# An attention-and-feed-forward chain on one core: another written-out order of all engines in the third stage

## The reference

```
hq, hk, hv = q @ Wq, k @ Wk, v @ Wv            # 16 heads of 64
attn = hq.hk + shift(hq.head_r) + hk.ub + shift(head_r.vb)   # content + relative part
attn = softmax(where(mask, -INF, attn / sqrt(128)))
out = (attn @ hv) * sigmoid(q @ head_w)
out = out @ Wo + q ;  out = layernorm(out) * ln_g + ln_b
```

## The kernel before, in words

| block | what | tile | line |
|---|---|---|---|
| hq0, hq1 | queries of heads 0-7, 8-15 | 128x128 | L1189, L1221 |
| hk0, hk1 | keys of heads 0-7, 8-15 | 128x128 | L1177, L1321 |
| hv0, hv1 | values | 128x120 | L1232, L1181 |
| z, xnT | head gate; transpose of the normed x | 128x128 | L1280, L1329 |
| rel 0..3 | relative scores of head pairs 0-1, 2-3, 4-5, 6-7 | 64x32 | L1244, L1274, L1304, L1347 |
| content 0, 1 | queries times keys, heads 0-7, 8-15 | 64x128 | L1258, L1213 |
| T0, T1 | transposes of the probabilities, half the heads each | 64x120 | L1205, L1315 |
| av | probabilities times values, four groups | 120x64 | L1169, L1287, L1292, L1355 |
| y | output product, in two halves | 128x128 | L1195, L1227 |
| qT, acc | transpose and product of part 4, 16-bit | 128x128 | L1251, L1334 |

## Time and profile before

### The profile page before, as it was taken

The page is one execution under the profiler, slowest core; times in us unless marked ns, Lnnn a source line. Parts: engine busy times, 40 slices in busy tenths (PEclk is TensorE's granted clock), DMA queues, the critical chain, the costliest instruction groups (busy, mean ns, idle before and its releaser), DMA issues.

```text
span 460.4 us, 16745 instructions
## 1 busy us (share of the span) xinstructions
PE 428.4 (93%) x6147; PEld 317.8 (69%) x6147; DVE 384.3 (83%) x1316; ACT 370.7 (81%) x1467; POOL 252.8 (55%) x370
## 2 busy tenths in 40 slices
PE   8999999988779989799999999999999999999781
PEld 7556556555547768577887887888788778787570
DVE  5899999998468985489888989989898998988974
ACT  1999999989724564379899899899889989989961
POOL 4488888878935651023244444553654555355684
PEclk9999999999669999899999999999999999999987
DMA  7150000000000002777566565766746766476100
GB/s 216 51 192 22 14 12 6 10 7 8 1 2 1 0 2 69 190 193 186 127 160 150 126 165 123 161 147 140 180 108 159 155 144 163 120 180 148 29 7 23
DMA packets 54392, 44.88 MB, mean 97 GB/s; under 512 B 43952, under 2 KB 49328, under 8 KB 54320
## 3 DMA queue, kind: packets, MB, share of 16 engines
q1 hardware_dynamic: 53616, 43.59, 38.6%
q10 hardware_dynamic: 704, 0.32, 0.2%
HBM read 22.92 MB, written 20.97 MB: 95 GB/s over the span
## 4 chain that ended last, share of the span: by engine, by line
PE 78%; DVE 11%; ACT 4%; POOL 3%; DMA 1%; issue 1%; SPq 1%; POOLq 0%
PE PS L964 68%; PE PS L1161 4%; PE PS L980 2%; PE PS L1141 2%; POOL prob L307 1%; ACT prob L488 1%; DMA ctx<-in_ctxT 1%; DVE relw L709 1%; DVE nmax L666 1%; DVE nmax L668 1%; DVE relr L714 1%; PE PS L1086 1%; DVE nmax L640 1%; DVE qT L699 1%; DVE probT L647 1%
## 5 line engine op out<-in xcount | busy, mean ns | idle before, releaser
L351 POOL TENSOR_TENSOR prob<-prob,rsum 128x480 f32<-128x480 f32 x64 | 62.6, 989 | 70.7 <-DVE rsum L832 37.4
L488 ACT ACTIVATE prob<-prob,nmax 128x120 f32<-128x120 f32 x256 | 100.3, 414 | 0.0
L417 ACT ACTIVATE prob<-PS,nmax 128x120 f32<-128x120 f32 x256 | 89.4, 394 | 3.3 <-DVE nmax L731 2.9
L307 POOL TENSOR_TENSOR prob<-prob,rsum 128x480 f32<-128x480 f32 x64 | 62.5, 986 | 22.1 <-DVE rsum L704 12.4
L417 ACT ACTIVATION_READ_ACCUMULATOR prob<-PS,nmax 128x1 f32 x256 | 61.7, 241 | 0.0
L488 ACT ACTIVATION_READ_ACCUMULATOR prob<-prob,nmax 128x1 f32 x256 | 56.3, 220 | 0.0
L964 PE MATMUL PS<-rT,qv 64*32 64x152 f32 x2048 | 48.1, 297 | 2.4 <-ACT relw L567 2.4
L964 PE MATMUL PS<-ctx,wk 128*128 128x120 f32 x288 | 43.9, 289 | 2.3 <-DMA ctx<-in_ctxT 2.3
L964 PEld LDWEIGHTS PS<-xnT,wq 128*128 128x128 f32 x288 | 36.8, 191 | 9.3 <-issue 6.8
L964 PEld LDWEIGHTS PS<-rT,qv 64*32 64x32 f32 x2048 | 28.6, 106 | 20.6 <-issue 18.6
L964 PE MATMUL PS<-xnT,wq 128*128 128x128 f32 x288 | 42.5, 285 | 0.0
(11 more groups left out here) (195 smaller groups left out, 1100.6 us busy)
## 6 DMA issues: line engine op xcount, KB each, us to landing
rel_scratch<-relw SPq DMA_DIRECT2D x128, 152.0 KB, 2.7
relr<-rel_scratch SPq DMA_DIRECT2D x64, 240.0 KB, 4.3
ctx<-in_ctxT SPq DMA_DIRECT2D x32, 60.0 KB, 1.9
out_x<-fin SPq DMA_DIRECT2D x16, 64.0 KB, 2.2
x_all<-in_x SPq DMA_DIRECT2D x1, 640.0 KB, 7.1
wr<-in_wr SPq DMA_DIRECT2D x1, 512.0 KB, 5.0
wq<-in_wq SPq DMA_DIRECT2D x1, 512.0 KB, 3.7
wk<-in_wk SPq DMA_DIRECT2D x1, 512.0 KB, 4.5
```

Of the source, the lines that this page charges most:

```text
L307: return pool.tensor_tensor(pr, pr, cols(rsum[p], g, HG).unsqueeze(2).to_broadcast([S, HG, SK]), ALU.mult)
L351: return pool.tensor_tensor(pr, pr, cols(rsum[p], g, HG).unsqueeze(2).to_broadcast([S, HG, SK]), ALU.mult)
L417: last = act.activation(cols(prob[p], n, SK), cols(scores, q, SK), ACT.Exp, bias=nmax[p][:, n:n + 1], accum_out=ssum[p][:, n:n + 1])
L488: last = act.activation(cols(pr, n, SK), cols(pr, n, SK), ACT.Exp, bias=bias[:, n:n + 1], accum_out=total[:, n:n + 1])
```

## The change

Only `layer1` changes, on all five engines, and the number of steps in `run_steps`: the last one is now step 23. Per element PE does the same products with the same tiles. Their order in a step, and with it the number of times that the tile of one block differs from that of the block before, becomes:

| | blocks of one step, in order (element) |
|---|---|
| before | av last quarter (s-4); hk0 (s-1), hv1 (s-2), hq0 (s), y 1st (s-4); T0 (s-3); content 1 (s-2); hq1 (s), y 2nd (s-4), hv0 (s-2); rel 0; qT (s-6); content 0 (s-1); rel 1; z (s-1); av 1st half (s-3); rel 2; T1 (s-3); hk1 (s), xnT (s+1), acc (s-6); rel 3; av third quarter (s-3) |
| after | content 1 (s-2); qT (s-7), hq0 (s), y 1st (s-4); av 2nd half (s-4); hk1 (s-1), z (s-1), hv1 (s-2), hq1 (s), acc (s-7), y 2nd (s-4), xnT (s+1), hk0 (s-1), hv0 (s-2); rel 1, rel 0; T0 (s-3); content 0 (s-1); rel 2, rel 3; av 1st half; T1 (s-3) |

Semicolons stand where the tile changes: round the step that is 15 times before and 10 after with T to content (64x120 to 64x128) counted, 14 and 8 without. Banks are dealt out anew. The copy of keys of heads 8-15 goes from DVE to ACT; ACT's copy of xnT comes one step earlier; DVE norms x one step earlier; part 4 (qT, acc, the copy `fin`) runs on element s-7 instead of s-6 up to the copy, and its result is stored at s-8 instead of s-7. On SP the store of the result moves ahead of the load of the context. Core of the diff:

```diff
-            peeled(layer1, LOOPS[2][1], NB + 7)
+            peeled(layer1, LOOPS[2][1], NB + 8)
...
 # SP: order of the transfers in a step
                     shifted(t, p, 0)
+                t, p = s - 8, par
+                if on(t):
+                    out_at = held(sp, t * S * D)
+                    sp.wait_ge(F1["out"], t + 1)
+                    sp.dma_start(bass.AP(out.tensor, out_at, [[D, S], [1, D]]), fin[p][:, :]).then_inc(F1[f"stored{p}"], 16)
                 t, p = s, par
...
-                    sp.wait_ge(A1["relw1"], t + 1)
+                    sp.wait_ge(A1["relw0"], t + 1)
                     store(t, p, 0)
...
 # ACT
+                    act.wait_ge(A1["hq_ps"], 2 * t + 2)
+                    act.activation(cols(qv[p], 1, 512), PS[:, 2, :], ACT.Identity, bias=vbs_sb[:, :], scale=SCALE1)\
+                        .then_inc(A1["qv1"], 1)
...
+                t, p = s - 1, 1 - par
+                if on(t):
+                    after(act, A1["rsum"], 4 * t - 4)
+                    act.activation(ez[p][:, :], PS[:, 7, 0:H], ACT.Exp, scale=-1.0).then_inc(A1["ez"], 1)
+                    act.activation(cols(kT[p], 1, 4 * SK), PS[:, 5, 0:4 * SK], ACT.Copy).then_inc(A1["kT1"], 1)
...
+                    act.wait_ge(A1["rel_ps"], 4 * t + 1)
+                    act.activation(relw[p][:, 2 * WIN:4 * WIN], PS[:, 3, 0:2 * WIN], ACT.Copy)
+                    act.activation(relw[p][:, 6 * WIN:8 * WIN], PS[:, 4, 0:2 * WIN], ACT.Copy)\
+                        .then_inc(A1["relw1"], 1)
+                    act.wait_ge(A1["rel_ps"], 4 * t + 2)
+                    act.activation(relw[p][:, 0 * WIN:2 * WIN], PS[:, 1, 0:2 * WIN], ACT.Copy)
+                    act.activation(relw[p][:, 4 * WIN:6 * WIN], PS[:, 5, 0:2 * WIN], ACT.Copy)\
+                        .then_inc(A1["relw0"], 1)
...
 # DVE
-                    dve.wait_ge(A1["hk_ps"], 2 * t + 1)
-                    dve.tensor_copy(cols(kT[p], 1, 4 * SK), PS[:, 1, 0:4 * SK]).then_inc(A1["kT1"], 1)
...
 # PE
+                    pe.wait_ge(A1["probT3"], t + 1)
...
+                t, p = s - 1, 1 - par
+                if on(t):
+                    pe.wait_ge(A1[f"ctx_loaded{p}"], loads(t, p))
+                    freed(pe, (A1["probT3"], t - 2, t - 3), (A1["relw2"], t + 1, t))
+                    for m in range(4, 8):
+                        last = mm(PS[:, 5, (m % 4) * SK:(m % 4 + 1) * SK], cols(wk1_sb, m, 2 * DK), ctx_sb[p][:, :])
...
+                    pe.wait_ge(A1["kT0"], t + 1)
+                    freed(pe, (A1["relw1"], t + 2, t + 1), (A1["u"], t - 2, t - 3))
...
+                    pe.wait_ge(A1["relw0"], t + 1)
+                    for m in (4, 5):
...
+                    freed(pe, (A1["probT0"], t - 2, t - 3), (A1["kT0"], t, t - 1))
...
+                    for m in (6, 7):
```

More of the change, by code:

```diff
@@ new lines, in layer1 @@
+                t, p = s + 2, par
+                if on(t):
+                    if isinstance(t, int) and t < 2:
+                        dve.wait_ge(F0["xnT_ps"], NB)
+                    dve.wait_ge(A1["rstd"], t + 1)
+                    after(dve, A1["xn_kept"], t - 1)
+                    dve.tensor_scalar(xn[p][:, :], row(x_all, t), mv[p][:, 0:1], rstd[p][:, 0:1],
+                                      ALU.subtract, ALU.mult).then_inc(A1["xn"], 1)
+                    dve.wait_ge(A1["xn"], t + 1)
+                    dve.tensor_copy(row(xn_all, t), xn[p][:, :]).then_inc(A1["xn_kept"], 1)
@@ new lines, in layer1 @@
+                t, p = s - 1, 1 - par
+                if on(t):
+                    dve.wait_ge(A1["content"], 2 * t + 1)
+                    dve.wait_ge(A1[f"relr0{p}"], 2 * loads(t, p))
+                    dve.tensor_tensor(cols(prob[p], 0, HG * SK), PS[:, 3, 0:HG * SK], cols(relr[p], 0, HG * SK), ALU.add)\
+                       .then_inc(A1["added0"], 1)
+                    dve.tensor_tensor(cols(prob[p], 1, HG * SK), PS[:, 7, 0:HG * SK], cols(relr[p], 1, HG * SK), ALU.add)\
+                       .then_inc(A1["added1"], 1)
@@ L1207, in layer1 @@
-                if on(t):
-                    freed(pe, (A1["kT0"], t + 2, t + 1), (A1["added1"], t + 1, t))
-                    freed(pe, (A1["relw3"], t + 2, t + 1), (A1["added0"], t + 1, t))
-                    for m in range(4, 8):
-                        for e, bank in ((0, 7), (1, 6)):
-                            half_ = slice(e * DK, (e + 1) * DK)
-                            last = mm(PS[:, bank, (m % 4) * SK:(m % 4 + 1) * SK], cols(qu[p], m, S)[half_], cols(kT[p], m, SK)[half_])
-                    last.then_inc(A1["content"], 1)
@@ L1295, in layer1 @@
[L1295 to L1300 removed]
+                    for m in (0, 1):
+                        for e, bank in ((0, 1), (1, 5)):
                             half_ = slice(e * DK, (e + 1) * DK)
@@ new lines, in layer1 @@
+                    pe.wait_ge(A1["scaled0"], ready)
+                    pe.wait_ge(A1["scaled1"], ready)
+                    probs_transpose(p, 0, (6, 0)).then_inc(A1["probT_ps"], 1)
+                t, p = s - 1, 1 - par
+                if on(t):
+                    pe.wait_ge(A1["kT0"], t + 1)
+                    freed(pe, (A1["relw1"], t + 2, t + 1), (A1["u"], t - 2, t - 3))
+                    freed(pe, (A1["hv0"], t, t - 1), (A1["ez"], t + 1, t))
+                    for m in range(0, 4):
+                        for e, bank in ((0, 3), (1, 7)):
+                            half_ = slice(e * DK, (e + 1) * DK)
+                            last = mm(PS[:, bank, (m % 4) * SK:(m % 4 + 1) * SK], cols(qu[p], m, S)[half_], cols(kT[p], m, SK)[half_])
+                    last.then_inc(A1["content"], 1)
@@ L1342, in layer1 @@
                     for m in (6, 7):
-                        for e, bank in ((0, 6), (1, 5)):
+                        for e, bank in ((0, 6), (1, 0)):
                             half_ = slice(e * DK, (e + 1) * DK)
```

570 lines of the change are left out of this document (248 added, 322 removed), and 9 rows, old and new, of the table A1.

## The result

| | before | changed | ratio, 95% interval |
|---|---|---|---|
| first timing, medians of 20 and 20 runs | 464.91 | 459.73 (457.72 to 465.69) | 0.992, 0.989 to 0.995 |
| a later job, 17 and 6 runs | 464.98 | 459.92 (459.53 to 460.75) | 0.989, 0.984 to 0.994 |

The ratio is not the quotient of the two medians, from which it differs by up to 0.6 points (here 0.989 by the medians).

The account below looks back on a forecast made before the run. PE was taken to bound the kernel at 16.31 us a step. Full steps 8.5 plus filling 3.9, emptying 0, made 12.4 off 462.21, so 449.8; with the median 0.4 above, 450 us, range 441 to 458.

Parts of the forecast that it names:

- PE, 15.60 us a step: Steady step: PE's blocks in the new order sum to 15.60 us, 0.71 less, with bounds 15.45 and 15.75.
- The forecast of 8.5 us for the twelve steps: Full steps 4 to 15: twelve times 0.71 us saved, 8.5 us in all.
- ACT, 15.25 and not the bound: Steady step: ACT takes over a 0.50 us copy, 14.75 to 15.25, and fits under 15.60 with 0.35 to spare.
- The two points with 0.1 to 0.2 us in hand: ACT's window copies before content 0 and rel 3: just in time for PE; a miss costs that much a step.
- loses 0.66 ..., keeps some 1.2 us a step free: Steady step: DVE sheds the key copy, 0.66 us (about 0.56 in a packed queue), and has some 1.2 us free.
- POOL is half idle: nothing: Steady step: POOL, busy 8.32 of 16.32 us, was expected to cost nothing.
- SP and `relr1`: SP's queue: the second shifted half waits behind the context load, mostly covered; DVE can be a further 1.5 us late.
- Filling 3.9 and emptying 0: First steps 3.9 us less in sum; last steps 0, from -2 to +2.
- The wait for the second context: Step 1, PE before hk1: 3.05 us for 0.68 of work; hk1 moves to step 2, 5.4 us less, 0.8 back.
- the 1.7 that I allowed for waits that stay: Steps 2 and 3: first scores wait for relr and exponentials whatever PE does, so 1.7 us of saving is given back.
- partly eaten: Rival: the two thin points fail or relr1 costs DVE, 0.3 us a step, filling gives only 1: 456.5 us; chance 0.20.
- ACT becomes the bound: Rival: ACT's work plus remaining waits sets the step, 15.95 to 16.25 us, no gain, 458 to 461.5; 0.11 shared between no-change cases.

Follow-up runs that it names:

- e2: The changed kernel with only DVE's order within a step altered, masks and xf moved away from POOL's scalings: 459.61 us, ratio 0.987.
- e8: The changed kernel with e2's DVE order up to step 15 and its own order from step 16 on: 457.17 us, ratio 0.980.
- e1: The changed kernel with POOL scaling only the first of 120 columns of each head's probabilities, so not the whole computation: 451.77 us, ratio 0.970.
- e3: The changed kernel with the second copy of keys moved back from ACT to DVE, ahead of u: 467.68 us, ratio 1.006.
- e10: The changed kernel with only DVE's mask of set 1 moved ahead of the two reciprocals that release POOL's scaling: 455.91 us, ratio 0.980.
- e11: The changed kernel with mask 2 moved ahead of its reciprocals and xf behind the maxima of set 3, mask 1 left: 459.95 us, ratio 0.990.
- e14: e8 plus 22 idle PE products in the last waits, with ACT's eight window copies of step 2 cut to 8 of 304 columns: 454.00 us, ratio 0.976.
- e7: e2 plus a one-column 16-bit product inside a pair of rel in every step, two more tile changes: 460.84 us, ratio 0.995.

## Why the prediction was wrong, step by step

- **PE, 15.60 us a step: right.** 15.55 with part 4 (e2, e8); without it 15.42, where the same sum gives 15.34; 15.48 on average over twelve once DVE is out of the way (e1, e8). The forecast of 8.5 us for the twelve steps is 9.5 with that.
- **ACT, 15.25 and not the bound: right.** 15.08 in a full step, and no wait of PE for it there. The two points with 0.1 to 0.2 us in hand held in the full steps; in the filling, where there is no T between, they are waits of 0.6 to 1.0.
- **DVE, "loses 0.66 ..., keeps some 1.2 us a step free": this failed**, and with it **"POOL is half idle: nothing"**. I costed each engine by its own busy time with durations from the old order, and a duration is not a property of the instruction alone. DVE went from 14.39 to 15.28 us a step (172.69 / 12, 183.38 / 12) where that step of the prediction makes it 13.8 (14.39 - 0.56), and PE then waited for it. (The 1.2 free is a slip besides: 15.60 less 14.71 - 0.56 leaves 1.45.) Shown by e1, e2, e3, e8, e10 and e11: 5.7 us in the twelve steps.
- **SP and `relr1`: right.** DVE has no wait for them among the eight steps' waits.
- **Filling 3.9 and emptying 0: failed**, 2.4 more in place of 3.9 less. The wait for the second context is gone as forecast (2.30 in the earlier trace rows), but the 1.7 that I allowed for waits that stay was too little: PE idles for 4.7 us up to the mark as before, 3.6 of it for window copies (2.4 before), and e14 shows that shortening one only brings out the next, DVE's. In the emptying the granted clock is 0.80 against 0.89 before, and products in the waits win back 1.4 to 1.5 us. The remaining part is measured, not explained.
- **Rivals.** The time fits "partly eaten" (456.5) better than the forecast, but not its mechanism, a miss at the two thin points. "ACT becomes the bound" (458 to 461.5; its own terms give 461.9 at the upper end) named the right time and the wrong engine, so its hit is luck. None of them had DVE's operations grow; "partly eaten" had DVE only by `relr1`.

## What to carry to other kernels

When the order of several engines is rewritten, lay DVE's and POOL's timelines side by side and look at what stands beside what: a mask with two SBUF inputs, or a normalisation such as `xf` from SBUF to SBUF, belongs where POOL rests, and reductions and reads of PSUM belong where it works. An instruction that releases POOL should not be followed at once by one that POOL then blocks. Whether it is released at once depends on POOL's own queue, which in the first and last steps is another than in the full ones. And a faster steady state is worth its time only if the last steps keep theirs: give them an order of their own, and compare filling and emptying apart from the full steps.

## What the runs showed of the hardware that I had not expected

- A mask of 128x480 (two SBUF inputs) takes 649 ns alone and 1401 when started 0.09 us behind a POOL operation of 986 that reads and writes SBUF; row maxima of the same tile stay at 640, and so do operations that read PSUM (`qu` 720 beside POOL, 742 alone). It goes both ways: in the changed kernel POOL's second scaling of the pair takes about 1400 in place of 986, beside DVE's mask 2 and `xf`.
- Even an operation on 128x4 goes from 155 to 429 ns beside POOL's `uo` of 128x128, and a mask of the same shape as the slow ones stays at 644 where it starts first and POOL waits (its `uo` 0.82 in place of 0.46).
- In the emptying, TensorE was granted 0.50 after waits of 2.2 and 1.8 us between its products (e2, up to 413.1 and 425.3, then half clock from 426.2 on for 17.1 us), after 1.1 and 1.8 in the changed kernel (up to 417.6 and 429.8, then 430.4 to 437.2), and in e1, with the 1.8 alone, not before 440.3. In e7, with 2.0 and 1.8 (up to 416.5 and 429.8), it came from 416.5 to 419.9 and from 430.2 to 433.6: nearly the same waits do not always bring the same stretch.
